# Fused two-layer block in fp32 on one core: which PSUM banks the sorted expert tiles use, and when their rows are scattered

## What is computed

```python
# layer 0: four exponential scans over time, added and layer-normed; 8 dense experts, weighted by a router
z = einsum('btd,ed->bte', xn, W); m = gated_scan(sigmoid(lam_logit), z); h = z + m @ eta; attn = gamma*norm(h)+beta
mid = silu(gate) * up; out = einsum('ebtf,efd->ebtd', mid, Wd); ffn = einsum('bte,ebtd->btd', weights, out)
# layer 1
r = sigmoid(x @ Wr.T); k = x @ Wk.T; v = x @ Wv.T
state = cumsum(k * v / scale, axis=1) * scale
attn = groupnorm_over_time_and_channels(r * state) @ Wo.T
top_w, top_i = top_k(logits, 2)            # 2 of 8 experts for each token
ffn = sum over the two of softmax(top_w) * (x @ expert_w[top_i] + expert_b[top_i])
```

## Time and profile before

| | us |
|---|---|
| time, median of 3 runs | 427.22 (426.89 to 427.35) |
| the profiled execution: its time | 427.0 |
| its span | 425.3 |
| TensorE busy | 413.8 (97%) |
| VectorE busy | 344.0 (81%) |
| ScalarE busy | 182.6 (43%) |
| GpSimd busy | 168.9 (40%) |

### The profile page before, as it was taken

One profiled execution on the slowest core, in us unless ns is written; L12 is line 12 of the kernel. 1 busy time (PEld: TensorE's weight loads), 2 busy tenths in 40 slices (PEclk: granted clock), 3 DMA queues, 4 the chain that ended last, 5 costly groups with the idle time before them and its releaser, 6 DMA issues.

```text
span 425.3 us, 7364 instructions
## 1 busy us (share of the span) xinstructions
PE 413.8 (97%) x2456; PEld 360.6 (85%) x2456; DVE 344.0 (81%) x1073; ACT 182.6 (43%) x358; POOL 168.9 (40%) x196
## 2 busy tenths in 40 slices
PE   8999999999999999999999999999999999999992
PEld 6688888978889988878889989788889888999872
DVE  6799998898997678989966888899779666668785
ACT  4745454443263536342536143524462253524130
POOL 1556369642136102510154716010720064455662
PEclk9999999999999999999999999999999999999998
DMA  8992699970771220000021300000202933522278
GB/s 275 414 317 97 192 277 279 280 192 0 105 132 64 83 68 0 2 0 2 12 88 42 108 2 0 2 2 0 88 13 72 262 124 117 150 74 88 76 217 289
DMA packets 32453, 48.97 MB, mean 115 GB/s; under 512 B 2728, under 2 KB 26560, under 8 KB 31904
## 3 DMA queue, kind: packets, MB, share of 16 engines
q1 hardware_dynamic: 26128, 36.27, 28.0%
q0 software_dynamic: 5296, 11.42, 10.5%
q10 hardware_dynamic: 992, 0.81, 0.6%
HBM read 24.83 MB, written 23.66 MB: 114 GB/s over the span
## 4 chain that ended last, share of the span: by engine, by line
PE 81%; DVE 9%; DMA 4%; issue 2%; POOL 1%; ACT 1%; DVEq 0%; SPq 0%; POOLq 0%
PE D L740 25%; PE G L740 21%; PE U L740 21%; PE M L740 8%; DMA fetched<-returned 3%; PE D L771 1%; DVE mid_lo L1388 1%; PE M L890 1%; DVE mid L1511 1%; DVE rows L1525 1%; DVE carry_gain L1762 1%; PE M L865 1%; DMA rows<-x 1%; DVE gamma L1764 1%; PE M L763 1%
## 5 line engine op out<-in xcount | busy, mean ns | idle before, releaser
L740 PE MATMUL D<-w_hi,mid_hi 128*128 128x256 f32 x260 | 74.2, 285 | 0.2 <-DVE rows L1525 0.2
L740 PE MATMUL D<-w_hi,mid_lo 128*128 128x256 f32 x260 | 73.5, 283 | 0.0
L740 PE MATMUL D<-w_lo,mid_hi 128*128 128x256 f32 x260 | 73.5, 283 | 0.0
L1131 ACT ACTIVATE mid<-G 128x512 f32<-128x512 f32 x64 | 38.0, 596 | 69.7 <-PE G L740 44.3
L1511 DVE TENSOR_TENSOR mid<-mid,U 128x512 f32<-128x512 f32 x64 | 43.0, 684 | 22.7 <-PE U L740 10.2
L1525 DVE SCALAR_TENSOR_TENSOR rows<-D,weight,rows 128x256 f32<-128x256 f32 x128 | 54.0, 476 | 8.8 <-remote 6.3
L566 POOL TENSOR_TENSOR w_lo<-w_raw,w_hi 128x512 fp32r<-128x512 f32 x35 | 50.3, 1469 | 23.0 <-ACT w_hi L1098 12.2
L1098 ACT ACTIVATE mid_hi<-mid 128x512 fp32r<-128x512 f32 x64 | 39.9, 631 | 38.8 <-DVE mid L1511 37.0
L1388 DVE TENSOR_TENSOR mid_lo<-mid,mid_hi 128x512 fp32r<-128x512 f32 x64 | 49.4, 793 | 4.6 <-ACT mid_hi L1098 3.3
L740 PEld LDWEIGHTS D<-w_hi,mid_hi 128*128 128x128 f32 x260 | 49.7, 191 | 2.1 <-issue 1.3
L740 PE MATMUL G<-xT_hi,w_hi 128*128 128x512 f32 x126 | 50.2, 398 | 0.3 <-POOL w_lo L566 0.3
(11 more groups left out here) (360 smaller groups left out, 939.3 us busy)
## 6 DMA issues: line engine op xcount, KB each, us to landing
sorted_rows<-weighted SPq DMA_DIRECT2D x8, 1542.0 KB, 19.3
stage<-sorted_rows SPq DMA_DIRECT2D x31, 128.5 KB, 2.5
w_raw<-weights SPq DMA_DIRECT2D x2, 1280.0 KB, 14.9
w_raw<-weights SPq DMA_DIRECT2D x2, 1024.0 KB, 23.8
w_raw<-opposite POOLq DMA_DIRECT2D x2, 1024.0 KB
fetched<-returned SPq DMA_DIRECT2D x4, 512.0 KB, 7.2
rows<-x SPq DMA_DIRECT2D x7, 256.0 KB, 3.3
w_raw<-weights SPq DMA_DIRECT2D x2, 768.0 KB, 8.7
```

The source lines that it names most:

```text
L740: ins = nc.tensor.matmul(out_ap, a, b, start=(first and n == 0), stop=(last and n == 3 * len(pairs) - 1))
L1131: nc.scalar.activation(mid[:, c, :], GU[2 * c][:, :], ACT.Silu).then_inc(silu_ready, 1)
```

## The change

Four things, all in the last group:

1. Units from 4 on all use G1 or U1 for the transpose and D0 or D1 for the product. So r of both halves goes to G0, k of both to U0, and v to M1 (half 0) and M0 (half 1). Half 1 now waits on TensorE until half 0 has been read (`r_ready`, `k_used`) and for `logit1_read`.
2. The order on TensorE: transpose 9 and product 8 ahead of the logits, unit 10 ahead of half 0, units 11 and 12 between the halves, units 13 to 15 behind half 1, then pair 0, product 15, and pairs 1 to 15. Before, units 9 to 15 stood behind or between the halves with pairs 0 to 4 between units 11 and 15. The moments stand behind pairs 3 and 6 where they stood behind 6 and 9. ScalarE follows the same order.
3. VectorE: `unit_low(4)` stands between the two halves of `y_add`, `unit_low(9)` and `(10)` ahead of the gates, `unit_low(11)` behind the scan of half 0, and all pair additions behind the last unit.
4. Scatters: those of units 4 to 13 wait on GpSimd until the product of unit u+2 is done (`PACED`). Before, units 4 and 5 waited for that, 6 to 8 for r, k or v, and from 9 on only for their own eviction.

```diff
-WIDE_UNITS = range(4, 9)
+WIDE_UNITS = range(4, UNITS)
+PACED = {4: 7, 5: 8, 6: 9, 7: 10, 8: 11, 9: 12, 10: 13, 11: 14, 12: 15, 13: 16}
+        def late_v(h):
+            return MT[1 - h]
 def unit_banks(u):
-            return (GU[2 + u % 2] if u in WIDE_UNITS else MT[u % 2]), DN[(u + 1) % 2]
+            return GU[2 + u % 2], DN[u % 2]
 def return_rows(u):
-                if u in (4, 5):
-                    pool.wait_ge(unit_ps, u + 3)
-                elif u in (6, 7, 8):
-                    pool.wait_ge(rkv_ps, at(LAST, 6, 2 * (u - 6) + 1))
+                if u in PACED:
+                    pool.wait_ge(unit_ps, PACED[u])
 def project_rkv_half(g, h):
-                for name, bank in (("r", GU[2 * h]), ("k", GU[2 * h + 1]), ("v", DN[h])):
-                    if name == "v" and h == 0:
-                        router_end(M0, 1, g)
-                    if name == "v":
-                        pe.wait_ge(unit_evicted, WIDE_UNITS.stop - 1 + h)
+                for name, bank in (("r", GU[0]), ("k", GU[1]), ("v", late_v(h))):
+                    if h:
+                        pe.wait_ge({"r": r_ready, "k": k_used, "v": logit1_read}[name],
+                                   at(g, 1, 1) if name == "v" else at(g, KC, 1))
...
+                    if name == "r" and h == 0:
+                        router_end(M0, 1, g)
 def unit_product(u, owners):
-                if u in (WIDE_UNITS.stop, WIDE_UNITS.stop + 1):
-                    pe.wait_ge(v_used, at(LAST, KC, u - WIDE_UNITS.stop + 1))
 def expert_pair(g, job):
-                if job < 4:
-                    pe.wait_ge(k_used if job % 2 else r_ready, at(g, KC, c + 1))
+                if job < 2:
+                    pe.wait_ge(k_used if job else r_ready, at(g, KC, KC))
+                elif job < 4:
+                    pe.wait_ge(unit_lo_ready, UNITS - 3 + job)
 ...
+                    pe.wait_ge(down_added, at(g, 2 * E, 2 * E - 1))
+                    unit_product(4, owners)
+                    unit_transpose(6)
                     pe.wait_ge(down_added, at(g, 2 * E, 2 * E))
-                    unit_product(4, owners)
-                    unit(6, owners)
+                    unit_product(5, owners)
                     unit(7, owners)
                     unit_transpose(8)
                     transpose_y(g)
                     unit_product(7, owners)
-                    unit_product(8, owners)
+                    unit(9, owners)
                     pe.wait_ge(yT_lo_ready, at(g, KC, KC))
                     logits(g)
+                    unit(10, owners)
                     project_rkv_half(g, 0)
-                    unit_transpose(9)
+                    unit(11, owners)
+                    unit(12, owners)
                     project_rkv_half(g, 1)
-                    pe.wait_ge(logit1_read, at(g, 1, 1))
-                    unit_transpose(10)
-                    unit_product(9, owners)
-                    unit(11, owners)
-                    for u in range(12, UNITS):
-                        expert_pair(g, u - 12)
+                    for u in range(13, UNITS):
                         unit(u, owners)
-                    expert_pair(g, 4)
+                    expert_pair(g, 0)
                     unit_product(UNITS - 1, owners)
-XX```

The first place is VectorE's program at half 0 of r, k and v. `ln<-U,carry_gain` is the product with k, the next `ln<-ln` row that with v, the two `SCALAR_TENSOR_TENSOR ln<-small_in,ln` rows are the scan, `w_lo<-` with the bank's name is `unit_low`, and the `stage_` row behind it tells the unit (stage_56 is the buffer of units 0 and 8, stage_57 of 1 and 9, and so on). Before:

```order
L1534 TENSOR_TENSOR ln<-U,carry_gain 128x512 [waits rkv_ps]
L1538 TENSOR_TENSOR ln<-ln,D 128x512 [waits k_used,rkv_ps]
L1593 TENSOR_SCALAR top_w<-th 128x4 [waits th1_ready]
L1594 TENSOR_SCALAR top_w<-th 128x4
L1597 TENSOR_TENSOR picked<-hot,top_w 128x64 [waits chain_back]
L1599 TENSOR_TENSOR small_in<-picked 128x32 [waits chain_back]
L1534 TENSOR_TENSOR ln<-U,carry_gain 128x512 [waits rkv_ps,chain_back]
L1538 TENSOR_TENSOR ln<-ln,D 128x512 [waits k_used,rkv_ps]
L1388 TENSOR_TENSOR w_lo<-M,w_hi 128x512 [waits unit_ps,unit_hi_ready]
L1659 TENSOR_TENSOR w_raw<-stage_58,w_raw 128x2 [waits unit_loaded2,ids_made]
L1666 MEMSET yT_hi 1x512 [waits logitT_ps1]
L1667 MEMSET yT_lo 1x512
```

More of the change, by code:

```diff
@@ L928, in expert_pair @@
                 pair, t = job // TILES, job % TILES
-                c = (job % 4) // 2
                 if t == 0:
@@ L1318, in group @@
                     unit_out(7)
-                    unit_out(8)
+                    unit(9)
                     logits_out(g, 1)
+                    unit(10)
                     tanh_r_half(g, 0)
+                    unit(11)
                     tanh_gap(g)
-                    unit_high(9)
-                    unit_high(10)
-                    unit_out(9)
-                    unit(11)
+                    unit(12)
                     tanh_r_half(g, 1)
-                    for u in range(12, UNITS):
+                    for u in range(13, UNITS):
                         unit(u)
```

39 lines of the change are left out of this document (18 added, 21 removed).

## The result

The changed kernel takes 431.17 us (median of 4 executions, 430.98 to 431.43) against 427.06 (4, 426.58 to 427.35) for the kernel before, measured side by side: a ratio of 1.009, 95% interval 1.0064 to 1.0116. It is slower, and above the predicted range of 425.8 to 429.0.

A forecast was written before the change was run, and what follows sets the result against it. TensorE, 97% busy, and two tails bound it, the DMA tail later by 1.5 us. TensorE +1.8 and fetched rows at 419.3 put the additions' end at 421.4 against 421.16, +0.2 span: 427.4 us, range 425.8 to 429.0.

The forecast's parts named there:

- From there 11 scatters stand in a row at 1.28 us, and the last starts at 390.0 + 12.8 = 402.8: GpSimd from unit 10's scatter on: no gaps, last start 402.8 against 403.23, so the DMA tail only 0.4 us earlier.
- what I had called no change: Whole kernel: a difference of less than 0.2% (0.85 us) can't be told from no change; chance of same 0.48.
- `att_low` now ends well ahead of `project_o`: GpSimd's queue behind the scatters: `att_low` would end early enough that `project_o` on TensorE doesn't wait; no cost.
- TensorE, +1.8: TensorE up to its last matmul: waits for low parts summed, 0.35 - 0.1 + 1.0 + 0.5 + 0.25 - 0.2 = +1.8 us.
- product 14: TensorE behind half 1: product 14 waits for its low part, delayed by the scan on VectorE; 0.25 us.
- the -0.2: First `project_o` on TensorE: its wait for `att_low` goes with the moments three pairs ahead; gain 0.2 us.
- The end: Kernel's tail: last result ends at 420.1, fetched rows are there, additions end at 421.4 against 421.16; span 425.5.
- `fetched` in the chain: Sign in the changed profile: the prediction is wrong if the chain of waits still goes over `fetched`.
- D: Rival, slower by the scatters: GpSimd's last scatter lands 1.5 us later than forecast, end at 428.1; chance 0.06.
- The rule that I weighed there: GpSimd's scatters: it can't write DMA descriptors while VectorE holds their shared port in some modes; no term in the sum.
- C's mechanism: Rival, slower: a copy 1.5 us late holds a product TensorE waits for; TensorE +3.3, time 428.9; chance 0.26.
- The estimate of 2.6 us for the last store: Last store of 256 KB: about 2.0 us plus its bytes at 436 GB/s; by it the time would be 426.4.

The follow-up runs named there:

- e17: Changed kernel with the scatters of units 8 to 15 counted on a second semaphore of their own: 426.36 us, ratio 1.0018 to the kernel before.
- e12: Changed kernel without the scatter waits of units 9 to 13, e1 word for word, run again for a second profile: 432.90 us, ratio 1.0119.
- e1: Changed kernel with the scatter waits of units 9 to 13 taken out, those of 4 to 8 kept: 432.69 us, ratio 1.0136.
- e4: Changed kernel with the low parts of units 11, 13 and 14 moved earlier on VectorE: 428.32 us, ratio 1.0032.
- e16: Changed kernel word for word, run once more for a second profile: 429.95 us in one run.
- e10: Kernel before with 4 more direct DMAs issued by GpSimd at the start of the second group: 429.18 us, ratio 1.0034.
- e13: Changed kernel with 8 more indirect DMAs of GpSimd at the start of the second group: 436.89 us, ratio 1.0213.
- e15: Changed kernel with low parts of units 11, 13, 14 earlier, `att_low` ahead of `add_first`, and 8 more indirect GpSimd DMAs: 434.48 us, ratio 1.0169.
- e2: Kernel before with only the change's scatter waits (units 4 to 13 wait for the product of unit u+2): 431.66 us, ratio 1.0101.
- e14: Kernel before with 4 more indirect DMAs of GpSimd at the start of the second group: 430.36 us, ratio 1.0076.
- e9: Changed kernel with 8 more direct DMAs issued by GpSimd at the start of the second group: 432.20 us, ratio 1.0106.

## Why the prediction was wrong

**The step that failed** is "From there 11 scatters stand in a row at 1.28 us, and the last starts at 390.0 + 12.8 = 402.8". It started at 407.79. Of the 5.0 us: 0.7 since unit 10's scatter began at 390.72, 0.2 since it took 1.16, 1.6 for the wait of unit 13 on product 15, whose signal came late in that execution, and 2.5 for the gap ahead of the 29th scatter. The last is the systematic one: in e17, which has all of the change but not the gap, the last scatter starts at 402.84, the last additions end at 421.29 (forecast 421.4), the span is 424.7 and the ratio 1.0018, inside what I had called no change. My replay left out a gap that was in the trace of before, since its named releaser made it look like a wait that the change removes. So I set a row without gaps (402.8) against one of before that had 4.3 us of them (403.23), and took the later start of unit 10, 4.56 us, for nearly free. How near e17 comes to the forecast is in part luck: the kernel before took 425.51 beside it, 1.5 us less than beside the changed kernel, and its last store took 2.9 us where I had 3.6.

**"`att_low` now ends well ahead of `project_o`"** failed by the same step. I had named the queue (joins, `add_first`, `att_low`) and not drawn that its start is the last scatter's landing. It cost 2.07 us in one profile, 0.3 in another.

**TensorE, +1.8.** The places were right: products 6, 11 and 13 wait for their low parts, 6 at 364.70 as forecast; product 14, to which I gave 0.25, doesn't. Up to the last matmul of the pairs the forecast is 2.0, since the -0.2 comes behind it. The size there was 2.6 in the first profile, with product 11 held 1.5 us instead of 1.0, since ScalarE's copy for unit 10 held VectorE ahead of the gates; in e17 it is 416.00 - 414.20 = 1.8. What is left of e17's time over the kernel before, 0.85 us, wasn't taken apart. The kernel before still has its gap: without it its last scatter would start at about 397.41 + 3 x 1.28 = 401.2, an estimate from its own rows, and not at 403.23. So the change may well cost more against a kernel before with two counters than e17 shows.

**The end.** The chain goes over TensorE and VectorE, as forecast, and over `fetched` and GpSimd ahead of them, which was not; `fetched` in the chain was my own sign of being wrong. The half clock, 1.5 us, wasn't in my sum at all: an idle stretch on TensorE costs more than itself when the clock falls behind it.

**Rivals.** It came out on the side of D, to which I gave 0.06, with a last scatter 4.6 us later than before where D had it 1.0 later. The rule that I weighed there (the Trainium skill, SBUF — State Buffer, the two separate sides) isn't what did it: of the scatters from unit 10 on all but the first take 0.97 us in the first profile. C's mechanism, a signal late on the thin chain, is what e12 shows, and the first profile too: ScalarE's copy of product 15 starts at 399.43, though the product's matmuls start at 395.43. The estimate of 2.6 us for the last store, from the Trainium skill (DMA: Bandwidth & Descriptors, the anatomy of one DMA; the page gives it for DMAs that GpSimd issues, and this store is SyncE's), is too short here: the last five stores of the changed kernel took 3.2 to 3.7 us from issue to landing. In e1 and e12, whose fetched rows had come well before the stores, they took 2.2 to 2.5.

## What to carry to other kernels

A gap that stands at one place in a row of equal instructions is a cost of its own until its releaser is checked against what the instruction asks for in the code; a replay that leaves it out is wrong by its length. When the end of the kernel hangs on the last of a long row of indirect DMAs from GpSimd, try two semaphores instead of one; here it gave 3.1 us. When two tails end within a few tenths of a microsecond of each other, ask what both hang on before taking away either. The kernel before with two counters is the version to try next; it wasn't run here, and neither was e4 with two counters.

## What the runs showed of the hardware

- The 29th of 31 indirect DMAs of GpSimd counted on one semaphore (16 each) doesn't start until the 28th has landed: 1.16 to 1.31 us after its last packet, in all 19 profiles that count this way. With 16 and 15 on two semaphores there is no such gap. Whether it is the count of 28, what of the machine counts it, and whether direct DMAs do the same, isn't shown.
- When a load of 16 KB of instructions fell together with a scatter, three of the scatter's 48 packets came only when the load ended, 1.2 to 2.0 us behind the others (seven profiles; e16: 401.79, 403.31); what waits for the whole scatter is as late. That they are one engine's packets is concluded from their number.
- Behind an idle stretch of TensorE the granted clock fell to about half for some 3.4 us in six executions (1.9 us idle in e10, 2.1 in the changed kernel, 2.2 in e13, 2.6 in e15, 3.6 in e12, 4.2 in e2) and stayed at 1.00 in others (1.7 us in e4, 1.9 in e14, 2.0 in e1, 2.1 in e9). So the length of that stretch alone doesn't decide.
- VectorE's first addition in the tail took 1.48 us beside GpSimd's additions (kernel before and changed) and 0.69 when these were done (e17).
- The last five stores took 3.2 to 3.7 us from issue to landing in the changed kernel and 2.2 to 2.5 in e1 and e12; between them lies e17 with 2.5 to 2.9.
- A signal of TensorE can be given late while its next matmuls start on time: the increment for k of half 1 came at 386.66 in e1 and at 390.78 in e12.
